# Convolution with tiles of 64 rows and two halves of channels at once, in a kernel of two layers on one core

## The reference, cut

```python
x = L0_attn_x                                     # [16, 512, 128]
xn = layernorm(x)
x = x + attention(xn) * silu(ffn(xn))             # layer 0: 16 heads of 8

xn = layernorm(x)
# layer 1, first half: a long convolution over time, channel by channel
k = irfft(rfft(B) / rfft(A) + h_0)[:, :512]       # one kernel per channel
y = irfft(rfft(k, 1024) * rfft(xn, 1024))[:, :512]
# layer 1, second half: each token goes to the best 2 of 8 experts
logits = xn @ router_w.T
values, which = top_k(logits, 2)
weights = softmax(values)
mixed = sum(weights[k] * expert[which[k]](xn))    # 128 -> 512 -> gelu -> 128
x = x + y * silu(mixed)
```

## Time and profile before

| | |
|---|---|
| median of 3 runs | 1534.9 us (1532.25 to 1538.44) |
| the profiled execution | 1536.7 us, span 1534.4 us, granted clock 0.938 |
| PE busy over the span | 1291.5 us, 84% |
| DVE, ACT, POOL busy | 1011.4, 855.9 and 556.0 us |
| `route_and_convolve` | from 1012.1 us to 1209.3 us of the span |
| DMA issues of convolution tiles by SP | 15 and 15, 1024 KB each |

### The profile page before, as it was taken

The page is one execution under the profiler, slowest core; times in us unless marked ns, Lnnn a source line. Parts: engine busy times, 40 slices in busy tenths (PEclk is TensorE's granted clock), DMA queues, the critical chain, the costliest instruction groups (busy, mean ns, idle before and its releaser), DMA issues. The chain is left out here.

```text
span 1534.4 us, 29388 instructions
## 1 busy us (share of the span) xinstructions
PE 1291.5 (84%) x8092; PEld 662.9 (43%) x8092; DVE 1011.4 (66%) x2343; ACT 855.9 (56%) x1661; POOL 556.0 (36%) x543
## 2 busy tenths in 40 slices
PE   5889999999999999999989999648786399999970
PEld 2433433433343343343333344224343388888760
DVE  1878888888888888888867886133344145454447
ACT  0277777777777777777767775112122244444432
POOL 2112332342342334234224115354555244444440
PEclk9999999999999999999999997668898699999995
DMA  6323312212311331231221232368774122222219
GB/s 224 97 96 104 107 32 98 106 54 69 105 61 66 109 106 35 88 106 54 72 102 50 74 93 65 94 228 291 225 256 137 46 68 65 69 67 66 62 55 329
DMA packets 114374, 162.27 MB, mean 106 GB/s; under 512 B 17649, under 2 KB 52145, under 8 KB 113778
## 3 DMA queue, kind: packets, MB, share of 16 engines
q1 hardware_dynamic: 103554, 140.88, 28.4%
q0 software_dynamic: 8448, 17.58, 3.3%
q10 hardware_dynamic: 2288, 2.90, 0.6%
HBM read 104.20 MB, written 49.77 MB: 100 GB/s over the span
## 5 line engine op out<-in xcount | busy, mean ns | idle before, releaser
L774 DVE TENSOR_REDUCE row_max<-ps_max 128x2 f32<-128x1024 f32 x512 | 620.5, 1220 | 151.2 <-PE ps_max L1033 149.3
L983 ACT ACTIVATE probs<-ps_exp 128x512 f32<-128x512 f32 x1024 | 559.1, 602 | 228.7 <-PE ps_exp L1033 211.3
L1033 PE MATMUL ps_exp<-q_op,k_op 32*128 32x512 f32 x1024 | 319.2, 504 | 7.8 <-ACT probs L983 7.2
L1033 PEld LDWEIGHTS ps_exp<-q_op,k_op 32*128 32x128 f32 x1024 | 139.3, 184 | 360.3 <-ACT probs L983 312.5
L1115 PE MATMUL ps_y<-probs,v_aug 128*32 128x512 f32 x2048 | 280.7, 618 | 4.5 <-issue 4.5
L1033 PE MATMUL ps_max<-k_op,q_op 32*128 32x512 f32 x1024 | 253.9, 496 | 2.8 <-DMA k_op<-k_parts_scratch 2.1
L1553 ACT ACTIVATE hidden<-ps_h,b 128x256 f32<-128x256 f32 x268 | 118.2, 474 | 156.6 <-PE ps_h L1530 147.0
L1596 POOL DMA_INDIRECT y_scratch<-result,goes_to x134 | 128.5, 959 | 152.7 <-DVE result L1581 123.7
L315 POOL DMA_INDIRECT sorted_scratch<-rows,place x120 | 116.4, 970 | 99.7 <-ACT rows L229 38.0
L670 POOL TENSOR_TENSOR rstd<-var_eps,minus_half 128x4 f32<-128x4 f32 x32 | 32.9, 1027 | 321.8 <-DVE var_eps L769 321.8
L1537 PE MATMUL ps_o<-w,hidden 128*128 128x128 f32 x1072 | 131.8, 276 | 0.0
(11 more groups left out here) (185 smaller groups left out, 1472.0 us busy)
## 6 DMA issues: line engine op xcount, KB each, us to landing
q_op<-q_parts_scratch SPq DMA_DIRECT2D x16, 1024.0 KB, 5.6
k_op<-k_parts_scratch SPq DMA_DIRECT2D x16, 1024.0 KB, 8.5
q_op<-k_pad_scratch SPq DMA_DIRECT2D x15, 1024.0 KB
k_op<-k_pad_scratch SPq DMA_DIRECT2D x15, 1024.0 KB
unit_rows<-sorted_scratch SPq DMA_DIRECT2D x136, 66.0 KB
q_parts_scratch<-qk_split SPq DMA_DIRECT2D x16, 512.0 KB, 3.1
k_parts_scratch<-qk_split SPq DMA_DIRECT2D x16, 512.0 KB, 2.8
q_parts_scratch<-qk_split SPq DMA_DIRECT2D x16, 256.0 KB, 2.4
```

The source lines that it names most:

```text
L774: dve.tensor_reduce(row_max[group // 2][:, t, head:head + 2], ps_max[u][:, :, :], AX.X, ALU.max)\
L983: act.activation(probs[s % 2][:, i, :], ps_exp[i % 2][:, :], ACT.Exp).then_inc(exp_done, 1)
L1033: return pe.matmul(out, lhsT, rhs, start=True, stop=True)
```

## The change

- The tiles have 64 rows instead of 128 (`TROWS`), and each is used for two halves of channels: 4 channels c to c + 3 on partitions 0 to 63, and the channels 64 + c to 64 + c + 3 on partitions 64 to 127. Such an octet of channels is one unit of work o, 16 in all (`NO`); its tile is 1 MB. `TOEPS` falls to 2 buffers; product o writes both `ps_t` banks, with 4 blocks of 64 rows, 512, 448, 384 and 320 columns wide. The matmuls are 64 rows by 32 columns.
- Half of the stationary operands stand on the wrong partitions for that, so the stage first copies them across (`cross`, two copies of 64 by 2048 on ACT and two on DVE) into `other_half`.
- `by_time` has four buffers. The attention's operands of even batches are freed with `layer0`.
- 14 octets are spread over the 12 batches (one each, two in batches 9 and 15), 2 come behind them.
- The order on PE: `turn_x` of the first batch, then for each batch `score`, the product of an octet, `rank_tokens`, `turn_x` of the next batch, the turns of the octet before, and a second octet if there is one. On ACT `copy_x` and `fetch_rows` of the next batch are done a batch ahead.
- ACT loads the first two tiles only when `inverse` has landed. The experts' weights are loaded behind tile 4 of 16.
- `combine` keeps its second operand in the weights' memory.

```diff
-TOEPS = 4
-def load_toep(eng, dram, route, ops, q):
-    src = bass.AP(dram["k_pad"].tensor, CG * (KPAD + T) * q, [[1, 128], [KPAD + T, CG], [1, T]])
-    eng.dma_start(toep_of(ops, q), src).then_inc(route.toep_loaded[q % TOEPS], 16)
+NO = NQ // 2
+TOEPS = 2
+TROWS = 64
+TRAIL = 2
+def half(r):
+    return slice(TROWS * r, TROWS * r + TROWS)
+def channel(o, r, i):
+    return TROWS * r + CG * o + i
+def load_toep(eng, dram, route, ops, o):
+    for r in range(2):
+        src = bass.AP(dram["k_pad"].tensor, (KPAD + T) * channel(o, r, 0), [[1, TROWS], [KPAD + T, CG], [1, T]])
+        eng.dma_start(toep_of(ops, o)[half(r), :, :], src).then_inc(route.toep_loaded[o % TOEPS], 16)
...
@@ layer0, scalar
-            for q in range(2):
-                load_toep(act, dram, route, ops, q)
+            act.wait_ge(inverse_spread, 16 * B)
+            for o in range(2):
+                load_toep(act, dram, route, ops, o)
             from_side("proj", B - 1, (B - 1) % 2, side(B - 1, STEPS))
...
@@ route_and_convolve
-        by_time = [sb(f"by_time{p}", [128, T]) for p in range(2)]
+        by_time = [sb(f"by_time{p}", [128, T]) for p in range(4)]
+        other_half = [sb(f"other_half{odd}", [128, N_TOK // 2 // 128, TROWS]) for odd in range(2)]
...
+        def octets(b):
+            n, beside = b - ROUTED, NO - TRAIL
+            return range(beside * n // len(batches), beside * (n + 1) // len(batches))
+        trailing = range(NO - TRAIL, NO)
+        def cross(odd, r):
+            return other_half[odd][half(r), :, :], res.xn[half(1 - r), odd::2, TROWS * r:TROWS * r + TROWS]
...
@@ sync
-            for q in range(2, NQ):
-                wait(sp, convolved, q + 1 - TOEPS)
-                load_toep(sp, dram, route, ops, q)
-                if q == TOEPS - 1:
+            for o in range(TOEPS, NO):
+                sp.wait_ge(convolved, 2 * (o + 1 - TOEPS))
+                load_toep(sp, dram, route, ops, o)
+                if o == 2 * TOEPS:
                     weights.load(sp, dram)
@@ scalar
+            route.copy_x(act, banks, ROUTED)
+            for r in range(2):
+                act.activation(*cross(0, r), ACT.Copy).then_inc(crossed, 1)
+            route.fetch_rows(act, res, ROUTED)
             for b in batches:
-                qs = quads(b)
-                route.copy_x(act, banks, b)
-                reverse(qs[0])
-                reverse(qs[1])
                 route.exp(act, b)
-                for q in qs[2:]:
-                    reverse(q)
-                route.fetch_rows(act, res, b)
+                for n, o in enumerate(octets(b)):
+                    reverse(2 * o)
+                    reverse(2 * o + 1)
+                    if n == 0 and b + 1 < B:
+                        route.copy_x(act, banks, b + 1)
+                if b + 1 < B:
+                    route.fetch_rows(act, res, b + 1)
+            for o in trailing:
+                reverse(2 * o)
+                reverse(2 * o + 1)
@@ tensor
-                for u in range(2):
-                    for i in range(CG):
-                        last = pe.matmul(ps_t[p][32 * i:32 * i + 32, 0:T - 128 * u], res.xn[:, u::2, CG * q + i], toep_of(ops, q)[:, i, 128 * u:],
-                                         start=(u == 0), stop=(u == 1))
-                last.then_inc(convolved, 1)
+                blocks = 256 // TROWS
+                for u in range(blocks):
+                    for i in range(CG):
+                        for r in range(2):
+                            last = pe.matmul(ps_t[r][32 * i:32 * i + 32, 0:T - TROWS * u], stationary(r, u, channel(o, r, i)),
+                                             toep_of(ops, o)[half(r), i, TROWS * u:], start=(u == 0), stop=(u == blocks - 1))
+                last.then_inc(convolved, 2)
...
+            route.turn_x(pe, res, banks, ROUTED)
             for b in batches:
-                qs = quads(b)
-                route.turn_x(pe, res, banks, b)
-                convolve(qs[0])
                 route.score(pe, banks, b)
-                convolve(qs[1])
-                route.rank_tokens(pe, banks, b)
-                for q in qs[2:]:
-                    convolve(q)
-            turn(NQ - 1)
+                if b == ROUTED:
+                    pe.wait_ge(crossed, 4)
+                for n, o in enumerate(octets(b)):
+                    product(o)
+                    if n == 0:
+                        route.rank_tokens(pe, banks, b)
+                        if b + 1 < B:
+                            route.turn_x(pe, res, banks, b + 1)
+                    turns(o - 1)
+            for o in trailing:
+                product(o)
+                turns(o - 1)
+            turns(NO - 1)
             load_ends(pe)
@@ vector
+            for r in range(2):
+                dve.tensor_copy(*cross(1, r)).then_inc(crossed, 1)
...
             for b in batches:
-                qs = quads(b)
-                out(qs[0] - 1)
                 route.choose(dve, banks, b)
-                out(qs[0])
                 route.place_tokens(dve, banks, b)
-                for q in qs[1:-1]:
-                    out(q)
+                for o in octets(b):
+                    outs(o - 1)
...
@@ combine
-        y_second = [ops[b // 8][b // 4 % 2][:, b % 4, :].bitcast(FP32) for b in range(B)]
+        y_second = [weights.w1[:, b, :] for b in range(E)] + [weights.w2[:, b, :, :].rearrange("p f c -> p (f c)") for b in range(B - E)]
```

More of the change, by code:

```diff
@@ L1309, in route_and_convolve @@
         batches = range(ROUTED, B)
-        def quads(b):
-            n = b - ROUTED
-            return range(NQ * n // len(batches), NQ * (n + 1) // len(batches))
+        def octets(b):
[4 more added lines that the diff above has]
+            return other_half[odd][half(r), :, :], res.xn[half(1 - r), odd::2, TROWS * r:TROWS * r + TROWS]
         def fill(eng, experts):
@@ L1375, in turn, with turns @@
                 for t in range(TT):
[L1376 removed]
+                    last = pe.transpose(ps_b[q % 2][:, t, :, :, :].rearrange("p c b h -> p (c b h)"), by_time[q % 4][:, 128 * t:128 * t + 128], res.ident[:, :])
                 last.then_inc(time_turned, 1)
[L1379 to L1382 removed]
+            def turns(o):
+                if o >= 0:
+                    turn(2 * o)
+                    turn(2 * o + 1)
+            route.turn_x(pe, res, banks, ROUTED)
             for b in batches:
[L1385 to L1387 removed]
                 route.score(pe, banks, b)
[L1389 to L1393 removed]
+                if b == ROUTED:
[11 more added lines that the diff above has]
+            turns(NO - 1)
             load_ends(pe)
@@ L1413, in out, with outs @@
                 last.then_inc(spread, 1)
+            def outs(o):
+                if o >= 0:
+                    out(2 * o)
+                    out(2 * o + 1)
+            for r in range(2):
+                dve.tensor_copy(*cross(1, r)).then_inc(crossed, 1)
             route.clear(dve, [ROW_SETS - 1])
@@ L1448, in _ @@
             dve.tensor_copy(units[:, 1:], sums[1][:, :]).then_inc(units_ready, 1)
-            out(NQ - 1)
+            for o in trailing:
+                outs(o - 1)
+            outs(NO - 1)
             load_ends(dve)
@@ L1601, in _, with combine @@
                 pool.wait_ge(stored[i], 16 * total + 16)
-def combine(nc, res, dram, s_all, ops):
+def combine(nc, res, dram, s_all, weights):
     with ExitStack() as ctx:
@@ L1708, in build @@
         route = Routing(nc, ctx, early)
-        ops = [[ctx.enter_context(nc.sbuf_tensor(f"{n}{p}", [128, NG, T], FP32R)) for p in range(2)] for n in ("q_op", "k_op")]
+        ops = [ctx.enter_context(nc.sbuf_tensor(f"{n}_odd", [128, NG, T], FP32R)) for n in ("q_op", "k_op")]
         layer0(nc, res, dram, early, route, ops)
@@ L1714, in build @@
         experts(nc, res, dram, ends, weights)
-        combine(nc, res, dram, s_all, ops)
+        combine(nc, res, dram, s_all, weights)
 def kernel(**inputs):
```

32 lines of the change are left out of this document (15 added, 17 removed).

## The result

| | before | after |
|---|---|---|
| median, us (5 runs each, side by side) | 1532.6 (1529.9 to 1538.4) | 1544.7 (1541.6 to 1547.0) |
| ratio | | 1.007, 95% interval 1.0052 to 1.0089 |
| profiled execution, us; its span | 1536.7; 1534.4 | 1547.0; 1545.2 |
| granted clock, whole span | 0.938 | 0.926 |
| matmuls | 8092 | 8604 |

The change makes the kernel 12 us (0.7%) slower. The forecast was 1540, slower by 5.

A forecast was written before the change was run, and what follows sets the result against it. Bound: behind each train of scatters TensorE gets some 67 matmuls through in 11.4 us. Last train at 1181.7 plus 32.5 gave 1214.2 against 1209.3, + 4.9 us; 1534.9 + 4.9 = 1540 us, range 1506 to 1568.

The forecast's parts named there:

- Tail of layer0: Before the stage: held-back tile loads let the last spread land in 3.4 us, not 7.8, giving back 4.4 us.
- Crossed halves: Stage start: two copies each on ScalarE and VectorE, 3.6 us per engine, ahead of the first product; first train about 1020.
- Product: TensorE in the stage: an octet costs 3.1 us against 3.6 for two quads, if the row halves run beside each other.
- rival 4: Product on TensorE: the two halves don't run at once, an octet takes 5.9 us; 1552 us in all; chance 0.08.
- Period: From one train of scatters to the next: the sum gives 13.9 us, 14.3 taken; 62 to 72 matmuls in 11.4 us.
- The double one: The period that holds a second octet (batch 9): 18.7 us, from adding 3.1 and 1.3 to a single period.
- Last train: End of the row scatters in the stage: the last train starts at 1181.7 instead of 1184.2.
- Tail: From the last train to the experts' first DMA: 32.5 us, before 25.1, with three products and five octets of turns left.
- Rival 1: Behind each train, TensorE's slow phase goes by time, not by number of matmuls: 1521 us; chance 0.18.
- Rival 2: Behind each train, TensorE's slowdown vanishes with the halved tile traffic and POOL is last: 1485 us; chance 0.10.
- the trickle: Behind each train TensorE gets some 67 matmuls through in 11.4 us and is free only from there to the next.
- Rival 3: Over the stage, TensorE's clock falls to its lower level, granted about 0.7: 1565 us; chance 0.12.

The follow-up runs named there:

- b_split: The kernel before with each matmul of a product cut into two of half the columns: 1557.4 us, ratio 1.017.
- b_late: The kernel before with only ScalarE's first tile loads held back behind the spread of the inverses: 1527.8 us, ratio 0.9989 (0.9967 to 1.001).
- w: The changed kernel with whole tiles of 128 rows and no crossed halves, the rest of the change kept: 1525.1 us, ratio 0.9947.
- rank-first: w with the rank's matmuls moved from behind both quads of the octet to between them: 1523.3 us, ratio 0.9946.
- w_gap: w with two small powers on POOL (2 x 1.03 us) behind the fourth of eight scatters in each train: 1509.2 us, ratio 0.9857.
- w_gap1: w with a pause of one power of 1.03 us on POOL behind the fourth scatter, in place of two: 1525.5 us, ratio 0.9924.

## Why the prediction was right, point by point

- **The size:** the forecast was 4.9 us slower, and the kernel is 11 to 12 us slower: the direction came out, and the forecast had less than half of the size. The stated range, 1506 to 1568, holds the times of three of the four rivals too, so that the time alone says little; what speaks for the mechanism are the parts below and the experiments.
- **Tail of layer0:** 3.4 us expected, 3.6 measured; the stage starts at 1007.1 (expected 1007.8). Right.
- **Crossed halves:** ScalarE 3.84 us (expected 3.6), VectorE 2.48 (expected 3.6, from a memset, which was the wrong neighbour: a copy of 2048 elements took 1.22). The first train at 1020.6 (expected 1020): ScalarE's two copies were what the first product waited for.
- **Product:** 3.12 us undisturbed (expected 3.1); rival 4 (5.9) fell. The Trainium skill, "TensorE: Matmul & The Clock Gate", Part 3, has row and column tiles compose; the trace agrees.
- **Period:** mean of ten 14.45 (expected 14.3), with 70 to 83 matmuls in the 11.4 us, mean 74.7, a few more than the 62 to 72 expected (only the train with the second octet beside it is above the 80 named as the point of doubt). That the mean is so close is in part luck: the sum gave 13.9, and 0.4 was added by choice. In the trace VectorE gets the rank 11.7 to 13.2 us behind the train, mean 12.5, where the sum had 12.3, and from there to the next train it is 1.96 us, where it had 1.6. The double one took 20.2 (expected 18.7): its rest behind the 11.4 us was reckoned at full clock, and was granted 0.69.
- **Last train:** 1185.2 (expected 1181.7): 0.6 + 10 × 0.15 + 1.5.
- **Tail:** 32.9 us (expected 32.5), two errors that offset each other. ScalarE's last copies ended 23.3 us behind the train and not 21.4: TensorE stood idle for 4.0 us ahead of product 14, since the late signal held up ScalarE's copies, and that product, at a granted 0.60, took some 5 us (1197.9 to 1202.9) in place of 3.1. Against that the four fills took 3.7 us and not 5.05. What is left, 6.0 us for the register loads (1212.14 to 1218.15), is the value that was chosen between 0 and 9, so that it was luck in part.
- **The sum:** the experts' first DMA comes 8.7 us later than before, expected 4.9. The other 2.1 us of the spans' difference lie behind it, in stretches whose instructions are the same (325.0 and 327.1 us); kernels with the code of before took 323.5 (b_split) to 328.0 (b_late) there, so that it is put down to the executions.
- **Rival 1 (time, not count)** fell by b_split, and with it the result that a hidden cost of instructions would have had. **Rival 2 (the trickle goes with the tile traffic)** fell by w, whose periods are the same at any traffic, and by the changed kernel's own periods. **Rival 3 (the clock)** holds in part: the granted clock over the stage fell from 0.85 to 0.74, near its point of 0.7, and the 1.5 us of the double period and the 1.9 of product 14 go with granted clocks of 0.69 and 0.60; the 25 us that it was given didn't come. What the clock costs in the single periods was not tested apart. **The chances:** those named for "slower than 1542.6" add up to 0.41 and not to 0.39.

The step on which all hung, that the number of matmuls behind a train sets the period, is shown from three sides: no trains, more matmuls, fewer matmuls. Its number, 67, was too narrow: 67 in before, 75 in the changed kernel and 80 in b_split. So was its wording: instructions of another engine seem to take from the same share. And it made little of a second half, which w, rank-first and the pause showed: with few enough matmuls the late signal sets the period. In w it is 4.3 to 7.5 us late, and when it arrives goes by the train, mostly 2.5 to 2.6 us behind the start of the last scatter, not by the work. With whole tiles the new order is faster than before (0.9947); halved tiles, which double the product's matmuls, made it slower (1.007).

## What to carry to other kernels

Where an engine issues dense rows of indirect DMAs, count instructions beside them, not only time: a product cut into twice as many matmuls of half the depth took 3.12 us alone, no more than two whole ones of 1.81, and cost some 17 us in the eleven periods here. Look for signals that arrive long behind the instruction that sends them (`remote` in a wait, with the sender done 5 us earlier), and place the end of such a row where nobody waits for it: a pause of 2.1 us, which makes each train longer, made w some 14 us faster. Test a restructured kernel with the disturbance taken away, to see whether it only meets something else, and then look at each period rather than at the mean: one wait for a tile made 5.8 us look like 8.0.

## What the runs showed of the hardware

- Behind the start of a train of eight indirect DMAs (1.26 us from one to the next), after some 5 to 8 us, matmuls of 0.17 us come one to four at a time, 0.7 us and more apart. In w, signals of TensorE whose matmuls were through 4.3 to 7.5 us before reached VectorE 2.5 to 2.6 us behind the start of the last scatter; in w_rankfirst most did so too, but three came 0.9 to 1.1 us behind it. A distance of 3.4 us in the middle of a train lets them through (w_gap); one of 2.3 us does so only where the train itself begins 2.3 us or more behind the one before (w_gap1).
- With 40 more waits on an idle ScalarE, seven or eight matmuls fewer got through in those 11.4 us (mean 67.1 in place of 74.7, one trace each).
- A copy of 64 partitions by 2048 fp32 took VectorE 1.22 us and ScalarE 1.91.
- 64 records of matmuls of 64 rows by 32 columns (1664 columns in sequence) on four column groups and two row halves took 3.12 us at a granted clock of 1.00.
- What it is that the engines share in the slow phase stays open; no view of the trace names it.
